# Cross-attention of 16 batches: K, V and Q projections moved from a stage of their own into the attention turns, each tile in two parts

## The chip, the cores and the metric

One NeuronCore of a Trainium2 chip runs the whole kernel. Its engines are TensorE (PE, whose weight loads are shown as PEld), VectorE (DVE), ScalarE (ACT) and GpSimd (POOL); SyncE (SP) issues nearly all DMAs. The metric is the device time of one execution in microseconds (us), the median of several.

## What is computed

```python
q = split_heads(x @ w_q)                     # x: 16 x 256 x 320, 20 heads of 16
k, v = split_heads(text @ w_k), split_heads(text @ w_v)   # text: 248 tokens of 512
out_text = softmax(q k^T / 4) v
out_ip   = softmax(q k_ip^T / 4 + mask_ip) v_ip           # the last 8 tokens, with a mask from boxes
out = (merge(out_text) + merge(out_ip)) @ w_out + b_out + x
```

All is float32. The large projections are computed as three products of rounded parts (high x high, low x high, high x low).

## The kernel before, in words

**Projections.** The 16 batches are taken as 8 groups of two (512 columns). A group has ten tiles, 0 to 9: three of K (`k_tile`, L628, 12 matmuls of 512 columns), four of V (`v_tile`, L636, 12 of 320), three of Q (`q_tile`, L642, 8 of 512). `three` (L624 to L627) issues the three products of a chunk, and there are four chunks of the 512 context channels. The inputs arrive by DMA (`load_c`, `load_x`) and are split into a high part on ACT (`split_c` L406, `split_x` L411) and a low part on DVE (L513, L517, L519). A finished K or Q tile is split the same way (ACT L417, DVE L525) and a V tile is copied out (ACT L425, L427); SP stores them to DRAM. The tiles of this stage rotate over five PSUM banks (`ring`). After group 0 come the eight special tokens of all batches (`special`, L694), and on DVE the box mask (`mask`, L484 to L500, 22 small instructions in a chain), which POOL stores (L375) to `aux_rows`.

**Attention.** Then come turns, one for each batch b, of ten pairs of heads, p = 0 to 9. In pair p of turn b PE issues the key scores of batch b (`key_scores`, L716, into the two banks `score_t`), the query scores of the *next* batch (`query_scores`, L666, into `score_q`, two banks for even and two for odd pairs), at even p the product with V for a group of four heads (`values`, L730, bank `pv`), at odd p from 3 on a piece of the output projection of batch b-1 (`project_out`, L739, bank `pj`). ACT takes the exponential of the key scores (L471), and after even pairs it copies `pv` out (L462). DVE takes row maxima of the query scores (`maxima`, L534 and L536); the maxima go through DRAM (`store_rows`, `load_rows`) and come back as rows of the stacked q operand before the key scores of that batch. DVE also turns and inverts the sums (L586, L589), turns back (L594), and adds the residual (L601); POOL scales (L387, L392).

**What sets the order.** Every engine runs its own list, written by hand, with waits on semaphores. Each engine's `batch` function is the list of a turn; the tables `VALUES`, `EVACUATE`, `INVERT`, `TURN_BACK`, `OUT`, `FINISH` say at which pair what is done. Batches 2 to 13 and groups 1 to 6 are loops (`Fori`). The ten query scores of batch 0 stand between the tiles of the last group (`FIRST_SCORES`). The stacked operands of a batch (`load_stack`, seven DMAs, L278, L281, L285) are loaded two turns ahead into one of three buffers.

```python
            def key_scores(t, p):
                if p % HALF == 0:
                    pe.wait_ge(rows_loaded[p // HALF], 16 * (t.b + 1))
                need(pe, exp_done, PAIRS * t.b + p)
            ...
            def values(b, u, k):
                need(pe, o_evac, QUADS * b + k)
                pe.wait_ge(exp_done, PAIRS * b + 2 * (k + 1))
```

## Time and profile before

| | |
|---|---|
| runs, median (lowest to highest) | 556.62 us (554.52 to 559.1), 3 runs |
| the profiled execution | 556.4 us, of which the span in the trace is 554.6 us |
| mean granted clock of TensorE | 0.972 |
| busy share of the span: PE, DVE, ACT, POOL | 87%, 69%, 51%, 23% |
| DMA | 112.49 MB, 203 GB/s over the span |

A busy share is an average over stages: the first third of the span is nearly all PE, the rest is shared between PE, DVE and ACT. The profiled execution was 1.8 us longer than its span and lies at the median of the runs.

### The profile page before, as it was taken

What the parts mean: (1) busy time and instruction counts of PE and PEld (TensorE: products, weight loads), DVE (VectorE), ACT (ScalarE), POOL (GpSimd) and SP (SyncE); (2) the same over time, 40 slices, a digit from 0 to 9 for tenths busy, and PEclk for the clock granted to TensorE, in tenths of its full rate; (3) what the DMA queues carried; (4) which work ended last, traced back from release to release, by engine and by line L of the source; (5) the groups of instructions that cost most, each with busy time, mean ns of one, the idle gap of its engine ahead of it and who ended that gap; (6) DMA issues with size and microseconds to landing.
All of it is one profiled execution on the core that took longest, in us unless ns stands there. A gap on an engine that the chain in (4) does not pass through costs nothing.

```text
span 554.6 us, 12517 instructions
## 1 busy us (share of the span) xinstructions
PE 481.5 (87%) x4304; PEld 323.7 (58%) x4304; DVE 384.9 (69%) x706; ACT 280.3 (51%) x355; POOL 127.9 (23%) x205
## 2 busy tenths in 40 slices
PE   3979899999999586799799889897987988989985
PEld 2868687887887463455455555554554555555542
DVE  2739425325325256899779989897997999999932
ACT  3633335344344013666556666565664666666671
POOL 6014000000000000432323332331332433332341
PEclk9989999999999787999979999999998999999999
DMA  8978888888788935672681762672754654763211
GB/s 271 362 266 149 259 298 273 309 268 293 272 261 270 345 120 179 200 243 74 204 261 33 247 221 89 234 233 79 235 170 154 219 154 144 245 204 103 72 52 47
DMA packets 94195, 112.49 MB, mean 203 GB/s; under 512 B 14304, under 2 KB 72992, under 8 KB 94144
## 3 DMA queue, kind: packets, MB, share of 16 engines
q1 hardware_dynamic: 93296, 109.89, 60.6%
q0 software_dynamic: 848, 1.90, 1.9%
q8 instruction: 33, 0.54, 0.4%
q14 instruction: 18, 0.15, 0.1%
HBM read 73.17 MB, written 38.63 MB: 202 GB/s over the span
## 4 chain that ended last, share of the span: by engine, by line
PE 48%; DMA 15%; issue 11%; SPq 10%; DVE 9%; ACT 4%; POOL 3%; DVEq 0%; ACTq 0%; POOLq 0%
PE pv L730 10%; DMA max_rows<-row_buf 10%; PE score_t L716 5%; PE pj L739 4%; PE score_q L666 3%; ACT probs L471 3%; SPq L278 3%; PE score_t L625 3%; PE score_t L626 3%; PE score_t L627 3%; SPq L285 2%; PE pj L625 2%; DMA q_stack<-max_rows 2%; PE pj L627 2%; PE pj L626 2%
## 5 line engine op out<-in xcount | busy, mean ns | idle before, releaser
L534 DVE TENSOR_REDUCE max_cols<-score_q 128x4 fp32r<-128x992 f32 x160 | 187.1, 1170 | 46.4 <-PE score_q L666 41.1
L471 ACT ACTIVATE probs<-score_t 128x1024 f32<-128x1024 f32 x160 | 163.4, 1021 | 72.0 <-PE score_t L716 71.9
L730 PE MATMUL pv<-probs,v_cur 128*32 128x256 f32 x1920 | 124.5, 394 | 0.6 <-ACT probs L471 0.6
L387 POOL TENSOR_TENSOR o_turned<-o_turned,inv_cols 128x256 f32<-128x256 f32 x80 | 49.8, 622 | 179.7 <-DVE inv_cols L589 179.7
L716 PE MATMUL score_t<-q_stack,k_stack 64*128 64x256 f32 x440 | 56.5, 335 | 29.4 <-ACT probs L471 17.6
L730 PEld LDWEIGHTS pv<-probs,v_cur 128*32 128x32 f32 x1920 | 55.3, 111 | 41.1 <-issue 4.6
L462 ACT ACTIVATE o_all<-pv 128x512 f32<-128x512 f32 x80 | 47.8, 598 | 60.7 <-PE pv L730 60.7
L716 PEld LDWEIGHTS score_t<-q_stack,k_stack 64*128 64x128 f32 x440 | 33.8, 189 | 74.8 <-ACT probs L471 37.7
L739 PE MATMUL pj<-wo_sb,o_all 128*128 128x320 f32 x192 | 69.0, 468 | 2.9 <-DVE o_all L594 2.2
L381 POOL TENSOR_TENSOR x_all<-x_all,bias_sb 128x640 f32<-128x640 f32 x16 | 24.9, 1554 | 192.5 <-DMA x_all<-in_x 192.5
L586 DVE STREAM_TRANSPOSE o_turned<-o_all 128x512 f32<-128x512 f32 x80 | 56.1, 702 | 11.9 <-ACT o_all L462 11.9
L666 PE MATMUL score_q<-k_stack,q_stack 64*128 64x256 f32 x440 | 47.2, 293 | 12.1 <-DVE max_cols L536 7.0
L513 DVE TENSOR_TENSOR stack<-o_all,stack 128x1024 fp32r<-128x1024 f32 x16 | 19.0, 1222 | 54.3 <-ACT stack L406 54.3
L666 PEld LDWEIGHTS score_q<-k_stack,q_stack 64*128 64x128 f32 x440 | 35.7, 195 | 15.0 <-DVE max_cols L536 6.9
L739 PEld LDWEIGHTS pj<-wo_sb,o_all 128*128 128x128 f32 x192 | 31.1, 188 | 18.7 <-DVE o_all L594 3.9
L392 POOL TENSOR_TENSOR o_all<-o_turned 128x128 f32<-128x128 f32 x80 | 36.7, 459 | 9.3 <-POOL o_turned L387 5.5
L716 PE MATMUL score_t<-stack 64*128 64x256 f32 x200 | 25.2, 330 | 10.6 <-ACT probs L471 7.0
L716 PEld LDWEIGHTS score_t<-stack 64*128 64x128 f32 x200 | 15.0, 184 | 31.3 <-ACT probs L471 16.1
L536 DVE TENSOR_REDUCE max_cols<-score_q 128x4 fp32r<-128x32 f32 x160 | 28.8, 180 | 0.0
L417 ACT ACTIVATE qk_out<-score_t 128x512 fp32r<-128x512 f32 (+1 forms) x24 | 13.9, 593 | 24.8 <-PE score_t L627 14.4
L625 PE MATMUL pj<-stack,wk_hl 128*128 128x512 f32 x32 | 13.8, 430 | 11.4 <-DVE stack L513 11.4
L525 DVE TENSOR_TENSOR qk_out<-score_t,qk_out 128x512 fp32r<-128x512 f32 (+1 forms) x24 | 15.8, 681 | 9.6 <-ACT qk_out L417 9.6
(134 smaller groups left out, 719.5 us busy)
## 6 DMA issues: line engine op xcount, KB each, us to landing
q_stack<-q_parts SPq DMA_DIRECT2D x33, 320.0 KB, 4.5
k_stack<-k_parts SPq DMA_DIRECT2D x33, 320.0 KB, 5.6
v_rows<-v_out SPq DMA_DIRECT2D x32, 320.0 KB, 2.4
v_cur<-v_rows SPq DMA_DIRECT2D x16, 640.0 KB
o_all<-in_ctxT SPq DMA_DIRECT2D x16, 512.0 KB, 5.2
q_parts<-qk_out SPq DMA_DIRECT2D x32, 256.0 KB, 2.5
k_parts<-qk_out SPq DMA_DIRECT2D x32, 248.0 KB, 4.7
x_all<-in_x SPq DMA_DIRECT2D x16, 320.0 KB, 3.3
```

Of the source, the lines that this page charges most:

```text
L387: pool.tensor_tensor(out, out, inv_cols[:, k, :].unsqueeze(2).broadcast_to([P, 2 * S // 32, DH]), ALU.mult).then_inc(scaled, 1)
L392: pool.tensor_tensor(o_norm_t[:, k // 2, :, half:half + DH], out[:, 0:S // 32, :], out[:, S // 32:, :], ALU.add).then_inc(o_added, 1)
L462: nc.scalar.activation(o_raw[:, k, :], pv[:, :], ACT.Copy)\
L471: nc.scalar.activation(probs[:, slot(u, p), :], score_t[:, :], ACT.Exp, scale=SCALE)\
L534: nc.vector.tensor_reduce(out=max_cols[:, h, :, at:at + 4:2].rearrange("p t e -> p e t"), in_=both[:, :, :, 0:TEXT], op=ALU.max, axis=AX.X ...
L536: nc.vector.tensor_reduce(out=max_cols[:, h, :, at + 1:at + 4:2].rearrange("p t e -> p e t"), in_=both[:, :, :, TEXT:KEYS], op=ALU.max, ax ...
L586: nc.vector.transpose(turned_blocks(k), o_raw[:, k, :].rearrange("p (j n) -> p j n", n=32))\
L625: mm(out, w_hi, x_hi_, start=start, stop=False)
L666: last = mm(score_bank(first, p, e)[:, tile * KEYS:(tile + 1) * KEYS], q_cols(w, p, e, tile * P, P), k_cols(w, p, e, 0, KEYS), start=True, ...
L716: last = mm(score_t[:, 512 * e + S * tile:512 * e + S * tile + S], k_cols(t.w, p, e, tile * P, P), q_cols(t.w, p, e, 0, S), start=True, st ...
L730: last = mm(pv[32 * t:32 * t + 32, at:at + S], values_of(u, kind, 4 * k + t), probs[:, slot(u, 2 * k + t // 2), a:a + S], start=kind != 1, ...
L739: last = mm(pj[:, 0:D], o_norm[:, u, c, t * P:t * P + P], wo_sb[:, c, :], start=c == 0, stop=c == OC - 1)
```

## The change

- **Alone stage.** Only tiles 0 to 14 (group 0, and K and the first two V tiles of group 1) are still projected ahead of attention, over the five banks. On DVE the mask now stands behind tiles 10 to 12 and not ahead of them.
- **Turn -1.** A new turn of ten pairs without key scores holds the query scores of batch 0 and tiles 15 to 19.
- **Hosting turns.** Turns -1 to 11 host five tiles each: an even turn the three K tiles and two V tiles of group (t + 4) / 2, the odd turn after it the other two V tiles and the three Q tiles. A tile's first two chunks are issued at the end of an odd pair, its other two at the even pair that follows, ahead of `values`. A Q tile has three matmuls in its first part and five in its second. ACT and DVE take the tile one pair later (`tile_due`). The two c halves of the next group are split at pairs 6 and 8 (ACT) and 6 and 9 (DVE) of odd turns; x at pairs 3 and 4 of even turns.
- **PSUM.** Hosted tiles use two banks of `score_q`, so that the query scores have one pair of banks, not two, until pair 3 of turn 12: a query score then waits for the maxima of the pair before it.
- **SBUF.** c and x of groups 2 to 7 come through one buffer `raw` of 1536 columns: each of the three loads (c half 0, c half 1, x) waits until the one before it has been split. `c_hi` and `c_lo` have buffers of their own; `o_raw` and `o_turned` have three slots, not five.
- **SP.** A turn's list also has the tile stores and the c or x loads; the stack's K rows and Q rows are loaded apart. `load_rows` of the first half now stands behind the store of the turn's second tile.
- **Code.** All loops are unrolled.

```diff
+SLOTS = 3
+TILES = 10
+LONE = 15
+LAST_HOST = B - 5
...
-        def score_bank(first, p, e):
-            at = 512 * (e + (0 if first else 2 * (p % 2)))
+        def pair_at(b, p):
...
-            at = 0 if first else 1024 * (p % 2)
+        def score_pair(b, p):
+            at = pair_at(b, p)
             return score_q[:, at:at + 1024].rearrange("p (e t n) -> p e t n", e=2, t=2)
-        ring = [pj[:, :], pv[:, :], score_t[:, 0:512], score_t[:, 512:1024], score_q[:, 1536:2048]]
+        lone_banks = [pj[:, :], pv[:, :], score_t[:, 0:512], score_t[:, 512:1024], score_q[:, 1536:2048]]
+        host_banks = [score_q[:, 1024:1536], score_q[:, 1536:2048]]
+        def tile_bank(n):
+            return lone_banks[n % 5] if n < LONE else host_banks[n % 2]
...
+            return 0 <= b < B
+        def hosted(t):
+            return -1 <= t <= LAST_HOST
+        def tile_due(t, p):
+            if p % 2 == 0:
+                return None
+            n = 5 * (t + 4) + (p - 3) // 2
+            return n if (hosted(t) if p > 1 else hosted(t - 1)) else None
+        def tile_freed(eng, n):
...
+            def load_c(g, h):
+                if g < 2:
                     need(sp, c_split, 2 * g + h - 1)
-                    sp.dma_start(c_raw[:, 2 * h:2 * h + 2, :], rows(ctxT[h * 256:h * 256 + 256, bass.ds(g * GT, GT)]))\
-                        .then_inc(c_loaded[h], 16)
+                elif h == 0:
+                    need(sp, x_tail, g if g > 2 else 0)
+                    sp.wait_ge(c_split, 2 * g)
+                else:
+                    sp.wait_ge(c_split, 2 * g + 1)
+                sp.dma_start(c_raw(g, h), rows(ctxT[h * 256:h * 256 + 256, g * GT:(g + 1) * GT]))\
+                    .then_inc(c_loaded[h], 16)
...
+            sp.wait_ge(ksp_stored, 96)
+            sp.wait_ge(sp_stored, 16)
+            sp.wait_ge(aux_stored, 64)
+            load_stack_k(0)
+            load_stack_q(0)
+            lone(12, 14)
...
+                if t >= 0:
                     load_rows(t, 1)
-                if t.there(-2):
-                    store_out(b - 2)
-                load_residual(b, u)
+                if hosted(t - 1) or t == -1:
+                    store_tile(5 * (t + 4) - 1)
+                if host and t % 2 == 0:
+                    load_x(g)
+                if host and t % 2 and g + 1 < GROUPS:
+                    load_c(g + 1, 0)
                 if ahead:
-                    scored(t, 0)
-                    load_stack(t.to(2))
+                    need(sp, st_ready, PAIRS * t)
+                    load_stack_k(t + 2)
                 if next_:
-                    need(sp, pv_ready, QUADS * b)
-                    load_values(b + 1, 1 - u)
-                    store_rows(b + 1, 0)
-                    load_rows(t.to(1), 0)
-                    store_rows(b + 1, 1)
-            def store_out(b):
-                need(sp, out_done, OT * (b + 1))
-                sp.dma_start(rows(out[bass.ds(b * S, S), :]), out_sb[:, :, :]).then_inc(out_stored, 16)
-            batches(sp, batch, tail=False)
+                    need(sp, pv_ready, QUADS * t)
+                    load_values(t + 1)
+                if there(t - 2):
+                    store_out(t - 2)
+                if t >= 0:
+                    load_residual(t)
+                if host:
+                    store_tile(5 * (t + 4))
+                if ahead:
+                    load_stack_q(t + 2)
+                if next_:
+                    store_rows(t + 1, 0)
+                if host:
+                    store_tile(5 * (t + 4) + 1)
+                if next_:
+                    load_rows(t + 1, 0)
+                if host and t % 2 and g + 1 < GROUPS:
+                    load_c(g + 1, 1)
+                if host:
+                    store_tile(5 * (t + 4) + 2)
+                    store_tile(5 * (t + 4) + 3)
+                if next_:
+                    store_rows(t + 1, 1)
+            for t in range(-1, B):
+                batch(t)
...
+                    n = tile_due(t, p) if t >= 0 or p != 1 else LONE - 1
+                    if n is not None:
+                        tile(n)
...
+                    if hosted(t) and t % 2 and g + 1 < GROUPS and p in SPLIT_C_HI:
+                        split_c(g + 1, SPLIT_C_HI[p])
+                    if hosted(t) and t % 2 == 0 and p == SPLIT_X_HI:
+                        split_x(g)
+            batch(-1)
...
+            tile(10)
+            split_x(1)
+            tile(11)
+            tile(12)
+            mask()
+            dve.wait_ge(preset, 8)
...
+                    n = tile_due(t, p) if t >= 0 or p != 1 else None
+                    if n is not None:
+                        tile(n)
...
+                    if hosted(t) and t % 2 and g + 1 < GROUPS and p in SPLIT_C_LO:
+                        split_c(g + 1, SPLIT_C_LO[p])
+                    if hosted(t) and t % 2 == 0 and p == SPLIT_X_LO:
+                        split_x(g)
...
+                alone = pair_at((n - 1) // PAIRS, (n - 1) % PAIRS) == pair_at(b, p)
+                need(pe, max_done, n if alone else n - 1)
...
+                if chunks[0] == 0:
+                    if j == 7:
                         pe.wait_ge(x_tail, g + 1)
...
+                    if n < LONE:
+                        if n >= 5:
+                            tile_freed(pe, n - 5)
                     else:
-                        q_tile(g, n - 7, out)
-                    if isinstance(g, int) and g == GROUPS - 1:
-                        for p in FIRST_SCORES.get(n, ()):
-                            query_scores(Turn(0, 0), p)
-                if first:
-                    special()
+                        tile_freed(pe, n - (1 if n == LONE else 2))
...
+            for n in range(TILES):
+                tile(n)
+            special()
+            for n in range(TILES, LONE):
+                tile(n)
+            pe.wait_ge(ksp_lo, 3)
+            pe.wait_ge(vsp_done, 1)
...
-                            query_scores(t.to(1), p)
+                    if there(t + 1):
+                        query_scores(t + 1, p)
+                    if p % 2 == 0 and (hosted(t) if p else hosted(t - 1)):
+                        tile(5 * (t + 4) + p // 2 - 1, (2, 3))
...
+                    if hosted(t) and p % 2:
+                        tile(5 * (t + 4) + p // 2, (0, 1))
+            for t in range(-1, B + 1):
+                batch(t)
...
-FIRST_SCORES = {3: [0, 1], 4: [2], 5: [3], 6: [4], 7: [5, 6], 8: [7], 9: [8, 9]}
+SPLIT_C_HI, SPLIT_C_LO = {6: 0, 8: 1}, {6: 0, 9: 1}
+SPLIT_X_HI, SPLIT_X_LO = 3, 4
```

Three places of the order show it. **TensorE, pairs 7 and 8 of an attention turn, before** (`score_t` key scores, `score_q` query scores, `pj` output projection, `pv` values):

```order
L716 MATMUL score_t<-q_stack,k_stack 128x256 x4
L666 MATMUL score_q<-stack 128x256 x4
L739 MATMUL pj<-wo_sb,o_all 128x320 x2
L716 MATMUL score_t<-q_stack,k_stack 128x256 x4
L666 MATMUL score_q<-stack 128x256 x4
L730 MATMUL pv<-probs,v_cur 32x256 x12
```

and now, the same pairs from the output projection on, in an odd turn with a Q tile (L645 to L647 and L673, L674 write it into a bank of `score_q`):

```order
L762 MATMUL pj<-wo_sb,o_all 128x320
L645 MATMUL score_q<-x_hi,wq_hi 64x512
L646 MATMUL score_q<-x_hi,wq_lo 64x512
L647 MATMUL score_q<-x_lo,wq_hi 64x512
L739 MATMUL score_t<-q_stack,k_stack 128x256 x4
L689 MATMUL score_q<-stack2 128x256 x4
L645 MATMUL score_q<-x_hi,wq_hi 64x512
L646 MATMUL score_q<-x_hi,wq_lo 64x512
L647 MATMUL score_q<-x_lo,wq_hi 64x512
L673 MATMUL score_q<-x_hi,wq_hi 64x512
L674 MATMUL score_q<-x_hi,wq_lo 64x512
L753 MATMUL pv<-probs,v_cur 32x256 x12
```

The part of a tile stands between the output projection and the next key scores, and between the query scores and the values. **VectorE, pairs 5 to 7 of an attention turn, before** (`max_cols` maxima, `c_lo` the low part of c):

```order
L586 STREAM_TRANSPOSE o_turned<-o_all 128x512 [waits o_added,o_evac]
L589 RECIPROCAL inv_cols<-o_turned 128x16 [waits turned]
L534 TENSOR_REDUCE max_cols<-score_q 128x2x2 [waits sq_ready]
L536 TENSOR_REDUCE max_cols<-score_q 128x2x2
L601 TENSOR_TENSOR out_sb<-pj,x_all 128x320 [waits biased,out_ready]
```

and now, pairs 6 and 7 of an odd hosting turn:

```order
L558 TENSOR_REDUCE max_cols<-score_q 128x2x2 [waits sq_ready]
L560 TENSOR_REDUCE max_cols<-score_q 128x2x2
L613 TENSOR_TENSOR out_sb<-pj,x_all 128x320 [waits biased,out_ready]
L534 TENSOR_TENSOR c_lo<-raw,c_hi 128x1024 [waits c_high]
L558 TENSOR_REDUCE max_cols<-score_q 128x2x2 [waits sq_ready]
L560 TENSOR_REDUCE max_cols<-score_q 128x2x2
L549 TENSOR_TENSOR qk_out<-score_q,qk_out 128x512 [waits hi_done]
L598 STREAM_TRANSPOSE o_turned<-o_all 128x512 [waits o_added,o_evac]
L601 RECIPROCAL inv_cols<-o_turned 128x16 [waits turned]
```

The low split of c, which waits for ACT (`c_high`), stands ahead of the maxima of pair 7. **VectorE at the end of the alone stage, now** (`o_turned` the special keys, `qk_out` the low parts of tiles 10, 11, 12, then the first of the mask):

```order
L586 TENSOR_TENSOR o_turned<-score_q,o_turned 64x128 [waits ksp_hi]
L549 TENSOR_TENSOR qk_out<-pj,qk_out 128x512 [waits hi_done]
L538 TENSOR_TENSOR x_lo<-o_all,x_hi 128x1024 [waits x_high]
L540 TENSOR_TENSOR x_hi<-o_all,x_hi 64x512
L549 TENSOR_TENSOR qk_out<-pv,qk_out 128x512 [waits hi_done]
L549 TENSOR_TENSOR qk_out<-score_t,qk_out 64x512 [waits hi_done]
L512 TENSOR_SCALAR x_all<-x_all,boxes 16x256 [waits loaded_boxes]
```

Before, the mask's first instruction followed the special keys directly.

## Rows read from the trace of the kernel before

**Rows 1.** Windows by stage: us, busy (count) by engine, granted clock, DMA share, GB/s
```profile
42.70:180.70 138.00, 136.00 (x698) 111.21 (x696) 62.55 (x87) 55.06 (x83) 4.77 (x7) 1.00 0.84 266
...
186.00:211.70 25.70, 19.95 (x100) 15.04 (x102) 13.64 (x22) 3.28 (x6) 0.00 (x0) 0.81 0.59 202
...
233.70:525.20 291.50, 258.28 (x2970) 151.40 (x2970) 260.08 (x515) 177.68 (x210) 96.92 (x154) 0.98 0.53 172
525.20:554.60 29.40, 21.41 (x208) 11.04 (x208) 10.72 (x27) 13.27 (x16) 9.03 (x15) 0.99 0.15 48
```

**Rows 2.** Timeline of PE, an even and an odd pair: start us, duration us
```profile
342.54 0.51 PE L716 MATMUL score_t<-q_stack,k_stack 64*128 64x256 f32 x4 [0.96 <-ACT probs L471]
...
342.88 0.40 PE L666 MATMUL score_q<-k_stack,q_stack 64*128 64x256 f32 x4
...
343.21 1.50 PE L730 MATMUL pv<-probs,v_cur 128*32 128x256 f32 x24
...
344.64 0.50 PE L716 MATMUL score_t<-q_stack,k_stack 64*128 64x256 f32 x4
...
345.31 1.34 PE L739 MATMUL pj<-wo_sb,o_all 128*128 128x320 f32 x4
...
346.58 0.50 PE L716 MATMUL score_t<-q_stack,k_stack 64*128 64x256 f32 x4
```

**Rows 3.** Timeline of PE, first matmuls of two V tiles, then of two K tiles
```profile
98.86 0.31 PE L625 MATMUL pj<-wv_hl,stack 128*128 128x320 f32 x1
...
100.62 0.31 PE L625 MATMUL pv<-wv_hl,stack 128*128 128x320 f32 x1
...
107.88 0.40 PE L625 MATMUL pj<-stack,wk_hl 128*128 128x512 f32 x1
...
110.67 0.39 PE L625 MATMUL pv<-stack,wk_hl 128*128 128x512 f32 x1
```

**Rows 4.** Timeline of PE, last group: a V tile between two query scores
```profile
192.35 0.50 PE L666 MATMUL score_q<-k_stack,q_stack 64*128 64x256 f32 x4
...
192.78 0.42 PE L625 MATMUL pj<-wv_hl,stack 128*128 128x320 f32 x1
...
194.74 0.50 PE L666 MATMUL score_q<-k_stack,q_stack 64*128 64x256 f32 x4
```

**Rows 5.** Timeline: first matmul of tile 10, first and last instruction of the mask
```profile
42.73 0.39 PE L625 MATMUL pj<-stack,wk_hl 128*128 128x512 f32 x1
```
```profile
40.79 0.55 DVE L490 TENSOR_SCALAR x_all<-x_all,boxes 16x256 f32<-16x256 f32 x1
...
52.91 0.28 DVE L500 TENSOR_SCALAR v_cur<-x_all 16x256 f32<-16x256 f32 x1
```

**Rows 6.** First load of batch 0's stack (SP), and the query scores that waited
```profile
173.93 2.09 SPq L278 DMA_DIRECT2D q_stack<-q_parts  x3
...
186.01 0.79 PE L666 MATMUL score_q<-k_stack,q_stack 64*128 64x256 f32 x4 [5.12 <-DMA k_stack<-k_parts]
```

**Rows 7.** DMA issues: KB each, median us from issue to landing
```profile
o_all<-in_ctxT SPq DMA_DIRECT2D x16, 512.0 KB, 5.2
...
aux_rows<-v_cur POOLq DMA_DIRECT2D x2, 80.0 KB, 3.3
```

**Rows 8.** Groups of 80 to 180 us: the splits of c, count, busy, mean ns
```profile
L513 DVE TENSOR_TENSOR stack<-o_all,stack 128x1024 fp32r<-128x1024 f32 x10 | 11.8, 1222 | 38.0 <-ACT stack L406 38.0
L406 ACT ACTIVATE stack<-o_all 128x1024 fp32r<-128x1024 f32 x10 | 10.0, 1051 | 0.0
```

**Rows 9.** Timeline of attention: copy-out of pv, maxima of a pair, an exponential
```profile
344.86 0.60 ACT L462 ACTIVATE o_all<-pv 128x512 f32<-128x512 f32 x1 [0.74 <-PE pv L730]
...
345.35 1.02 ACT L471 ACTIVATE probs<-score_t 128x1024 f32<-128x1024 f32 x1
345.42 1.19 DVE L534 TENSOR_REDUCE max_cols<-score_q 128x4 fp32r<-128x992 f32 x1
346.53 0.18 DVE L536 TENSOR_REDUCE max_cols<-score_q 128x4 fp32r<-128x32 f32 x1
```

598 lines of the change are left out of this document (270 added, 328 removed).

## The prediction

> **What bounds the kernel now.** I read the windows by stage first [rows 1]. Three stages stand in them. From 42.7 to 180.7 us only projections run: PE is busy 136.0 of 138.0 us at clock 1.00, DVE and ACT under half. From 186.0 to 211.7 the last tiles and the first query scores share PE, which is busy 19.95 of 25.7 us at clock 0.81. From 233.7 to 525.2 run 14 attention turns, 291.5 / 14 = 20.8 us each, PE busy 258.3 of 291.5. So a PE-bound stage stands beside one where PE has gaps, and the change wants to fill the gaps with the tiles. What they are worth is read from the timeline of a pair [rows 2]. Key scores to query scores 0.34 us, query scores to values 0.33, values to the next key scores 344.64 - 343.21 = 1.43: an even pair is 2.10 us of PE. An odd pair with four matmul records of output projection is 1.94 (1.27 from 345.31 to 346.58). A turn's PE work is 10 x 0.67 + 5 x 1.43 + 12 records of output projection at 1.27 / 4 = 3.8, together 17.7 us. The turn takes 20.8: only 3.1 us of it are gaps.
>
> **Hosted work on PE.** A V tile is 100.62 - 98.86 = 1.76 us, a K tile 110.67 - 107.88 = 2.79 [rows 3], so 0.2325 for a matmul of 512 columns and 8 x 0.2325 = 1.86 for a Q tile. A group is 3 x 2.79 + 4 x 1.76 + 3 x 1.86 = 21.0, half a group in a turn 10.5 on average. A turn's last tile is finished in pair 0 of the next, so an even turn has the second part of a Q tile (5 x 0.2325 = 1.16), three K tiles, a V tile and half a V tile: 17.7 + 1.16 + 8.37 + 1.76 + 0.88 = 29.8 us. An odd turn has half a V tile, two V tiles, two Q tiles and the first part of a third (0.70): 26.5. So PE alone makes a hosting turn 28 on average, not 20.8. The gain has to come from the 138 us that vanish ahead of them.
>
> **What a part costs beyond its matmuls.** The trace has one place where a tile stands between scores: from a query score to the next with one V tile between, 194.74 - 192.35 = 2.39 us [rows 4]. Less 1.76 and less the 0.34 of query scores in rows 2, 0.3 is left for two changes between kinds of matmul, 0.15 for one. A part adds one net change to its pair. Ten parts: 1.5 us in each turn. Bounds: 0 (PE's queue hides it) and 0.3 for each, 3.0 a turn. I take 0.15, the nearest row.
>
> **The start.** Up to tile 10 nothing changes: 42.7 us [rows 5]. Tiles 10 to 14: 3 x 2.79 + 2 x 1.76 = 11.9, to 54.6. On DVE the mask now waits for tile 12, whose matmuls end at 42.7 + 8.4 = 51.1; its high and low copy cost about 0.6 and 0.8 (estimated from the 512-column copy of rows 9), so the mask starts near 52.6 and takes 53.2 - 40.8 = 12.4 [rows 5]: 65.0. Its two stores by POOL land 3.3 after issue [rows 7], about 1 us for the issues: 69.4. Only then SP may load batch 0's stack. Before, the first load issue and the first query score stood 186.0 - 173.9 = 12.1 us apart with a second stack's loads mixed in [rows 6]; alone I take 10 (bounds 7.5, the seven issues and one landing, and 12.1). Turn -1 starts at 79.5: PE stands still for 25 us. Before, this wait was hidden under six groups of tiles.
>
> **Turn -1.** With one pair of banks its clock is the loop query scores (0.4 to 0.8) and maxima, 346.71 - 345.42 = 1.29 [rows 9], with handovers near 2.0 us, ten times; two c splits of 1.2 on DVE [rows 8], and a clock that was 0.81 in the like stretch before [rows 1]. I take 22.5 (bounds 20 and 25.7): turn 0 starts at 102, where before it started at 211.7. That is 110 us earlier. In return 60 of the 80 tiles, 12 x 10.5 = 126 us of PE, lie in turns 0 to 11, which have gaps of 12 x 3.1 = 37 us for them.
>
> **The hosting turns.** Turn 0 has no values of an earlier batch and no output projection: 29.8 - 1.4 - 3.8 + 1.5 = 26. Turns 1 to 11 (six odd, five even): 6 x 26.5 + 5 x 29.8 + 11 x 1.5 = 324.5. On top come two waits, which I follow through the engines' lists. ACT and DVE take their lists in order.
> - Odd turn, pair 6: values end 0.67 + 1.16 + 0.15 + 1.43 = 3.4 us into the pair; ACT copies `pv` out (0.15 later, 0.6 [rows 9]), only then splits c (1.05 [rows 8]), to 5.2; DVE, at the head of whose queue the low split waits, ends it at 6.45. Behind it stand the maxima of pair 7, to 7.7, and for these the query scores of pair 8 now wait, as they have one pair of banks; they were due at 3.4 + (0.67 + 1.27 + 0.70 + 0.15) + 0.34 = 6.5. Cost 1.25.
> - Pair 8: the second half of c is loaded only after that split, issue near 6.6 and landing 5.2 later [rows 7], 11.8; ACT splits it to 12.6 or later, and the exponential of pair 9 (1.02) stands behind: key scores of the next turn at 13.75, due at 12.9. Cost 0.85. DVE's low split, then maxima: query scores of the next pair 1 late by 1.1.
> - Together 3.2 in each of the five odd turns that split (1, 3, 5, 7, 9): 16. Bounds: 0, if the slack of other pairs takes it, and 6 each (30), if landings take 3 us more. The x split in even turns comes out within 0.3 of its cover (load issued after the last Q tile's store, near 10 us into the turn, split due at 13.5): 1.5 in all.
>
> DVE and ACT by themselves have room: DVE's added work is (six lows of 0.7, two c splits, an x split) near 4.2 us a turn on about 18.5 of busy time, under 28.
>
> [...]
>
> **The end.** Turns 12 to 14 as before, 3 x 20.8 = 62.4; the last 29.4 [rows 1] unchanged.
>
> **Sum.** 102 + 26 + 324.5 + 16 + 1.5 + 62.4 + 29.4 = 561.8 of span, against 554.6; with the 1.8 us around the span 563.6, so 563. The profiled execution, 556.4, lies at the median of the runs, 556.6. Break-even is a mean of (554.6 - 102 - 62.4 - 29.4) / 12 = 30.1 us over turns 0 to 11; I have 368 / 12 = 30.7.
>
> **Rivals.**
> - *PE hides the waits.* The changes of kind cost nothing, and the c split's waits are taken by slack: and turn -1 takes 20.5: 563 - 16.5 - 16 - 2 = 528; with half of it true, 546. For it: 136.0 of 138.0 us busy in the dense stage, and waits of PE in the turns before were few. Against: rows 4, and the list order on DVE.
> - *The single raw buffer decides (slower).* c half 1 and x are loaded only when the part before is split, and the engines stand with exponentials and maxima behind them. With the landing at 8 us, not 5.2 and near 4 for x (stack loads, values and tile stores now share the DMA queues), each odd turn loses 3 more and each even turn 2.5: 5 x 3 + 5 x 2.5 = 27, 590; with half of it 577. It decides from a landing of about 5 us after issue. For it: 12.1 us for a stack in rows 6. Against: the DMA share would be near 0.7, below the 0.84 of the projection stage, where 5.2 was measured.
> - *The clock.* PE restarts after 25 us of rest, and turn -1 has it busy about 60%. If the low clock, 0.81 on average in rows 1, lasts through turn 0, it adds 5: 568.
> - *The change doesn't overlap at all* (a wait holds each tile until attention has finished its pair): turns of 20.8 + 10.5 = 31.3, 12 x 31.3 = 376 in place of 368: 571.
>
> **How the numbers follow.** Forecast, a little slower, 551 to 575: chance 0.46, near half of it within 1% of the median. First rival 0.32, all of it faster than 551. Raw buffer 0.16, slower. The last two together 0.06, a third of it within 1%. So faster by over 1% 0.32, within 1% 0.26, slower by over 1% 0.42; one per cent is about what runs of this kernel can tell from no change. Range 538 to 584: it leaves out the deep end of the first rival (528 to 538) and the deep end of the second.
>
> **What would show it.** Tile 14 ends near 54.6 and PE then waits for a DMA till about 79.5. Turn 0's key scores start near 102. Even hosting turns near 31, odd ones near 30, with PE or PEld waiting for maxima in pair 8, for an exponential in the next pair 0, and for maxima in pair 1. In pairs without split, PE waits for nothing. Wrong would be: a start of turn 0 beyond 108 or before 96; waits of ACT for `raw` of over 2 us; a mean hosting turn under 29 or over 32; a granted clock under 0.97 in turns 1 to 11.

## The result, and the profile after

The changed kernel takes 566.99 us (median of 4 runs, 564.82 to 570.51), the kernel before 557.42 beside it (554.52 to 559.1): ratio 1.022, 95% interval 1.016 to 1.027. It is slower by about 2%; the forecast was 563.0, range 538 to 584. The profiled execution took 566.87, its span is 565.1, its mean granted clock 0.96.

Windows of the changed kernel by stage answer to [rows 1]: us, then busy time (count) of PE, PEld, DVE, ACT, POOL, then granted clock, DMA share, GB/s.

```profile
54.60:79.50 24.90, 1.88 (x15) 1.64 (x13) 9.56 (x24) 0.96 (x2) 1.01 (x2) 0.58 0.41 125
79.50:99.60 20.10, 16.55 (x85) 11.22 (x85) 14.24 (x22) 2.90 (x5) 0.00 (x0) 0.84 0.80 271
99.60:128.90 29.30, 27.21 (x238) 17.23 (x237) 22.19 (x38) 16.72 (x22) 4.70 (x7) 1.00 0.70 218
128.90:466.50 337.60, 326.94 (x2921) 211.62 (x2921) 248.12 (x459) 180.06 (x236) 79.81 (x121) 1.00 0.67 212
466.50:491.70 25.20, 21.37 (x218) 11.97 (x218) 19.72 (x38) 13.22 (x17) 6.80 (x11) 0.93 0.58 181
491.70:533.70 42.00, 36.34 (x424) 21.43 (x425) 37.54 (x75) 25.35 (x30) 13.72 (x22) 1.00 0.40 125
533.70:565.10 31.40, 23.39 (x208) 11.87 (x208) 10.77 (x27) 13.27 (x16) 9.00 (x15) 0.87 0.14 44
```

The rows are the hole at the start, turn -1, turn 0, turns 1 to 11, turn 12, turns 13 and 14, and the end. In turns 1 to 11 TensorE is busy 326.9 of 337.6 us at a granted clock of 1.00: it is the bound there, as it was under the dense projections in [rows 1]. The lengths, each from the key scores of pair 0 to those of the next turn, against the forecast's terms:

| stretch | forecast | measured | difference |
|---|---|---|---|
| start of turn 0 | 102 | 99.6 | -2.4 |
| turn 0 | 26 | 29.3 | +3.3 |
| turns 1 to 11 | 324.5 + 16 + 1.5 = 342 | 337.6 | -4.4 |
| turns 12 to 14 | 62.4 | 67.2 | +4.8 |
| the last stretch | 29.4 | 31.4 | +2.0 |
| span | 561.8 | 565.1 | +3.3 |

The terms miss by 16.9 us in all, and by 3.3 after they cancel: that the sum lies so near is in part luck. Before, turns 12 to 14 took 20.56 + 19.68 + 19.78 = 60.0 us by the starts of their key scores, not the 62.4 of the mean turn, so against the kernel before they are 7.2 us longer, not 4.8.

The hole at the start, in the timeline of the changed kernel (start us, duration us, what it waited for): last step of the mask, SyncE's first stack load, its last, and the first query score.

```profile
64.69 0.28 DVE L522 TENSOR_SCALAR v_cur<-x_all 16x256 f32<-16x256 f32 x1
...
68.56 1.99 SPq L276 DMA_DIRECT2D k_stack<-k_parts  x3
...
72.60 0.62 SPq L272 DMA_DIRECT2D q_stack<-aux_rows  x1
...
79.46 0.80 PE L689 MATMUL score_q<-k_stack,q_stack 64*128 64x256 f32 x4 [23.02 <-DMA q_stack<-aux_rows]
```

The mask ends at 65.0 and the first query score comes at 79.46: forecast 65.0 and 79.5. Between them two small misses cancel: the stack load is issued at 68.6, not 69.4, and the query score comes 10.9 us after it, not 10. Before, the like load stood under a queue of projection tiles [rows 6]; now TensorE stands 23 us.

The waits that the forecast followed through the lists, in turn 1 (its pair 8 begins at 151.5, turn 2 at 159.0):

```profile
149.51 1.05 ACT L421 ACTIVATE c_hi<-raw 128x1024 fp32r<-128x1024 f32 x1
150.59 1.23 DVE L534 TENSOR_TENSOR c_lo<-raw,c_hi 128x1024 fp32r<-128x1024 f32 x1 [2.70 <-ACT c_hi L421]
151.74 1.19 DVE L558 TENSOR_REDUCE max_cols<-score_q 128x4 fp32r<-128x992 f32 x1
152.16 0.44 SPq L214 DMA_DIRECT2D raw<-in_ctxT  x1
153.07 0.50 PE L689 MATMUL score_q<-stack 64*128 64x256 f32 x4 [1.04 <-DVE max_cols L560]
...
159.03 0.50 PE L739 MATMUL score_t<-stack 64*128 64x256 f32 x4 [0.56 <-ACT probs L483]
160.92 1.16 DVE L534 TENSOR_TENSOR c_lo<-raw,c_hi 128x1024 fp32r<-128x1024 f32 x1
162.15 1.15 DVE L558 TENSOR_REDUCE max_cols<-score_q 128x4 fp32r<-128x992 f32 x1
...
163.46 0.50 PE L689 MATMUL score_q<-k_stack,q_stack 64*128 64x256 f32 x4 [0.51 <-DVE max_cols L560]
```

Read it from the DVE row at 150.59: VectorE stood 2.70 us for ScalarE's `c_hi` with the maxima of pair 7 behind it, and the query scores of pair 8, which have one pair of banks, then stood 1.04. The two other waits follow at pair 0 and pair 1 of the next turn, where the forecast had them. But the first of these does not come from the load, as the forecast had it. ScalarE's rows, and the load of `raw` (KB, us from issue to landing):

```profile
156.43 0.60 ACT L475 ACTIVATE o_all<-pv 128x512 f32<-128x512 f32 x1 [3.33 <-PE pv L753]
156.93 1.05 ACT L421 ACTIVATE c_hi<-raw 128x1024 fp32r<-128x1024 f32 x1
```
```profile
raw<-in_ctxT SPq DMA_DIRECT2D x1, 512.0 KB, 3.7
```

Issued at 152.16, the second half of c landed near 155.9. ScalarE waited for the values to copy `pv` out, split c right behind, and took the exponential of pair 9 after that. The load was in time; the copy-out of `pv` set the start, as it did at pair 6. Pairs by the starts of their key scores (us):

| pair | with c splits (turn 3) | without (turn 11) | cost | forecast |
|---|---|---|---|---|
| 8 | 4.76 | 3.46 | 1.30 | 1.25 |
| 9 | 2.74 | 2.10 | 0.64 | 0.85 |
| 1 of the next turn | 3.07 | 2.26 (run e3) | 0.81 | 1.1 |

The stretch that the forecast had wrong is turn 12, the first without tiles. Before, the last turns took 19.7 to 20.6 us; now turn 12 takes 25.2. Its rows in the changed kernel:

```profile
471.74 0.51 SPq L253 DMA_DIRECT2D q_stack<-max_rows  x1
472.78 1.15 SPq L239 DMA_DIRECT2D q_parts<-qk_out  x2
474.10 1.96 SPq L276 DMA_DIRECT2D stack<-k_parts  x3
...
477.18 0.40 SPq L297 DMA_DIRECT2D out<-out_sb  x1
...
484.45 0.49 DVE L613 TENSOR_TENSOR out_sb<-pj,x_all 128x320 f32<-128x320 f32 x1 [2.23 <-issue]
485.00 2.23 PE L762 MATMUL pj<-wo_sb,o_all 128*128 128x320 f32 x4 [2.41 <-DVE out_sb L613]
487.16 0.80 PE L739 MATMUL score_t<-q_stack,k_stack 64*128 64x256 f32 x4
```

SyncE issues the store of batch 10's output at 477.18, 10.7 us into the turn, behind a maxima load, the store of tile 79 and a stack load. VectorE's next residual sum writes the same `out_sb`; by its list it waits for that store, though the row names no releaser for its 2.23 us. It starts at 484.45, and the output projection stands 2.41 us for it. The key scores after the wait take 0.80, not 0.51, at a granted clock of 0.50 (window 487.0 to 488.0); over the turn it is 0.93, where it had been 1.00.

### The profile page after: what moved, and what is told of

It reads as the page before. It is cut to its first block, busy times and chain, and to the rows that moved or that the text cites. A ratio compares the mean times of both kernels' runs of the same rounds, so it can differ in the third digit from the quotient of the medians.

```text
span 565.1 us, 11048 instructions
## 1 busy us (share of the span) xinstructions
PE 495.4 (88%) x4304; PEld 321.7 (57%) x4304; DVE 385.0 (68%) x706; ACT 274.6 (49%) x355; POOL 131.8 (23%) x206
## 3 DMA queue, kind: packets, MB, share of 16 engines
q0 software_dynamic: 944, 2.23, 2.2%
## 4 chain that ended last, share of the span: by engine, by line
issue 56%; POOL 19%; PE 8%; DMA 6%; DVE 6%; SPq 3%; ACT 1%; POOLq 0%; ACTq 0%; DVEq 0%
POOL o_turned L402 9%; POOL o_all L407 6%; POOL x_all L396 4%; DMA probs<-in_wv_ip 3%; DVE max_cols L558 2%; PE score_q L689 1%; DMA v_rows<-v_out 1%; PE score_q L645 1%; DMA q_stack<-aux_rows 1%; DVE x_all L514 1%; PE score_q L646 1%; PE score_q L647 1%; DVE c_lo L534 1%; PE pj L762 1%; PE pv L753 1%
## 5 line engine op out<-in xcount | busy, mean ns | idle before, releaser
L753 PE MATMUL pv<-probs,v_cur 128*32 128x256 f32 x1920 | 120.4, 383 | 0.6 <-ACT probs L483 0.6
L402 POOL TENSOR_TENSOR o_turned<-o_turned,inv_cols 128x256 f32<-128x256 f32 x80 | 53.9, 674 | 165.9 <-DVE inv_cols L601 165.9
L762 PE MATMUL pj<-wo_sb,o_all 128*128 128x320 f32 x192 | 71.7, 484 | 5.9 <-DVE out_sb L613 3.9
L598 DVE STREAM_TRANSPOSE o_turned<-o_all 128x512 f32<-128x512 f32 x80 | 56.1, 701 | 11.8 <-ACT o_all L475 11.8
L762 PEld LDWEIGHTS pj<-wo_sb,o_all 128*128 128x128 f32 x192 | 32.2, 194 | 22.3 <-DVE out_sb L613 5.4
L645 PE MATMUL score_q<-wv_hl,c_hi 128*128 128x320 f32 x112 | 43.0, 384 | 0.0
L646 PE MATMUL score_q<-wv_hl,c_lo 128*128 128x320 f32 x112 | 35.1, 313 | 0.0
L647 PE MATMUL score_q<-wv_hl,c_hi 128*128 128x320 f32 x112 | 35.0, 312 | 0.0
L645 PE MATMUL score_q<-c_hi,wk_hl 128*128 128x512 f32 (+1 forms) x72 | 33.1, 460 | 0.0
L549 DVE TENSOR_TENSOR qk_out<-score_q,qk_out 128x512 fp32r<-128x512 f32 (+1 forms) x40 | 27.4, 684 | 7.3 <-ACT qk_out L442 5.8
L534 DVE TENSOR_TENSOR c_lo<-raw,c_hi 128x1024 fp32r<-128x1024 f32 x14 | 16.8, 1202 | 22.3 <-ACT c_hi L421 22.3
```

The costliest lines, as they stand in the source:

```text
L402: pool.tensor_tensor(out, out, inv_cols[:, n % SLOTS, :].unsqueeze(2).broadcast_to([P, 2 * S // 32, DH]), ALU.mult).then_inc(scaled, 1)
L598: nc.vector.transpose(turned_blocks(n), o_raw[:, n % SLOTS, :].rearrange("p (j n) -> p j n", n=32))\
L645: mm(out, w_hi, x_hi_, start=start, stop=False)
L753: last = mm(pv[32 * t:32 * t + 32, at:at + S], values_of(u, kind, 4 * k + t), probs[:, slot(u, 2 * k + t // 2), a:a + S], start=kind != 1, ...
L762: last = mm(pj[:, 0:D], o_norm[:, b % 2, c, t * P:t * P + P], wo_sb[:, c, :], start=c == 0, stop=c == OC - 1)
```

## The experiments

All times are medians of 4 to 10 runs, each with the kernel before on the same chip beside it. The changed kernel was not run again beside them, so of the timed runs the ratio to the kernel before (1.022 for the changed kernel) is what compares, and what a step is worth is read from the traces, one for each kernel. Each edit is to the changed kernel (567.0) unless it says e8.

**e1: the mask first.**

```diff
-            tile(10)
-            split_x(1)
-            tile(11)
-            tile(12)
-            mask()
+            mask()
+            tile(10)
+            split_x(1)
+            tile(11)
+            tile(12)
...
-            lone(7, 12)
+            lone(7, 10)
...
-            lone(12, 14)
+            lone(10, 14)
```

> Against the changed kernel at 567.0: the mask goes ahead of projected tile 10 on VectorE, and SyncE stores tiles 10 to 13 behind the first stack load instead of ahead of it. Theory A (the first query score waits 23 us for the stack load, which waits for the mask, and nothing else is behind it): the first query score comes 10 to 11 us earlier, near 69, and every later turn starts that much earlier: about 556.5 us. Rival B (turn -1 is then held by something else, the second ctxT load or tiles 10 to 14 evacuated late): turn -1 grows by about what the start gains, 563 to 567.

Measured: 557.64, ratio to before 1.002 (0.997 to 1.006); span 553.9.

```profile
68.15 0.80 PE L689 MATMUL score_q<-k_stack,q_stack 64*128 64x256 f32 x4 [11.78 <-DMA q_stack<-aux_rows]
```

The first query score comes 11.3 us earlier and the span falls by 11.2. Theory A, but the two numbers agree by luck: turn 12 starts only 8.3 us earlier, and of the rest 2.0 is the last stretch, 29.4 us here and 31.4 in the changed kernel, which the mask doesn't touch. Turn 0 gave back 2.3 us (31.6, not 29.3): ScalarE's second split of c still waited for its load (5.83 us, at 89.52), with an exponential and the maxima behind it. The mask and SyncE's order were moved together; between them they decide whether the changed kernel is slower or level.

**e2: one split a pair earlier.**

```diff
-SPLIT_C_HI, SPLIT_C_LO = {6: 0, 8: 1}, {6: 0, 9: 1}
+SPLIT_C_HI, SPLIT_C_LO = {5: 0, 8: 1}, {6: 0, 9: 1}
```

> One number changes: ScalarE's first split of c goes to pair 5 instead of pair 6; VectorE's stays at pair 6. Theory A (the long pair 8 of each odd turn, 4.76 against 3.46 without splits, comes from VectorE's low split standing 2.7 us for ScalarE's high one, with the maxima behind it): that wait is gone, pair 8 of the odd turns 1 to 9 falls to about 3.5, the second half of ctxT is loaded some 2 us earlier, and the time falls by 5 x 1.3 = 6.5 to 8 us, to about 560. Rival B (ScalarE itself is the late one: its exponential of pair 6 moves behind the split and takes the wait over): pair 6 or 7 grows by about 1 us and the time stays within 2 us of 567.

Measured: 564.84, ratio 1.012 (1.003 to 1.020). Pair 8 of the odd turns fell from 4.76 to 3.46, just as theory A said; but pair 9 rose from 2.74 to between 2.85 and 3.14 (3.86 in turn 9), and turn 0 from 29.3 to 32.0. The wait named by theory A was real: with VectorE's split still at pair 6, it was ScalarE's place alone that took it away. Of the 6.5 us, pair 9 of the five turns took back 2.4 and turn 0 another 2.7. Neither theory had the number.

**e3: no splits.** Loads and splits of c and x return at once for groups 2 and up, with the waits for them.

> Leaves out, from group 2 on, the loads and the splits of ctx and x; every later projected tile is made from group 1's values, so this is a time only. Theory A (the splits cost their waits, 16 us in the odd turns and 1.5 in turn -1 and the even turns, as forecast): about 549.5 us, hosted turns all at 29 to 29.5. Rival B (TensorE is the bound and hides the splits; the odd turns with a split, 29.95, are only 2 us longer than turn 11 without one, 28.0): 5 x 2 + 5 x 0.5 = about 12 us less, 555. Rival C (their loads also hold up other transfers): under 545.

Measured: 548.97, ratio 0.983 (0.975 to 0.992). Window of turns 1 to 11 in this run:

```profile
126.10:449.90 323.80, 323.80 (x2922) 210.88 (x2921) 228.26 (x439) 163.85 (x221) 75.58 (x121) 1.00 0.60 193
```

TensorE is busy 323.80 of 323.80: without splits and their loads it waits for nothing, so all of the difference to 337.6, 13.8 us, is the price of the two there. Another 2.8 is in turns -1 and 0. Odd turns take 28.0 and even ones 31.1 here; the forecast had 28.0 and 31.3. Theory A in size.

**e4: stores ahead in turns 12 to 15.**

```diff
+                if not host:
+                    store_out(t - 2)
+                    load_residual(t)
                 if t >= 0:
                     load_rows(t, 1)
...
-                if there(t - 2):
+                if host and there(t - 2):
                     store_out(t - 2)
-                if t >= 0:
+                if host and t >= 0:
                     load_residual(t)
```

> In the turns without projected tiles (12 to 15) SyncE stores the output of two turns ago and loads the residual before it loads maxima rows and stacks; nothing else moves. Theory A (turn 12 takes 25.2 us, not 20.8, because the late store of out_sb holds VectorE's residual sum, and with it the output projection, for 2.4 us, and the clock falls behind that wait): turn 12 falls to 21 to 22, the total by 3 to 4.5, to about 563. Rival B (turn 12 is long because of projected tile 79 and the single pair of score banks in its first pairs): turn 12 stays above 24 and the total within 1.5 us of 567.

```profile
471.20 0.38 SPq L297 DMA_DIRECT2D out<-out_sb  x1
...
467.80:490.10 22.30, 19.81 (x218) 11.26 (x217) 20.56 (x41) 13.22 (x17) 6.92 (x11) 1.00 0.66 204
```

The store goes out 3.4 us into the turn; turn 12 takes 22.3 us, not 25.2, at clock 1.00, and turn 13 takes 19.75, not 22.2, without a wait of 1.97 us for maxima rows at its end. Turns 12 to 14 together take 61.8 us, 5.4 less. The span is 560.7, 4.4 less, for turn 12 started 1.3 us later in this execution. Store and residual load were moved together. The timed median, 565.19 (ratio 1.016, 1.004 to 1.027), fell by less, and its interval holds both 0 and 4.4: the mechanism is shown by the trace, its size only there.

**e5 and e6: whole tiles.** The parts (2, 3) and (0, 1) become one call for all four chunks, in e5 at the even pair, in e6 at the odd pair.

```diff
 # e5
-                        tile(5 * (t + 4) + p // 2 - 1, (2, 3))
+                        tile(5 * (t + 4) + p // 2 - 1)
...
-                    if hosted(t) and p % 2:
-                        tile(5 * (t + 4) + p // 2, (0, 1))
```

> Each projected tile is made whole at the even pair where its second part stood; the odd pairs carry none. Theory A (a change of kind of matmul costs TensorE 0.15 to 0.2 us, as the forecast had it, and there are five fewer of them per hosted turn): 12 turns x 0.75 to 1.0 = 9 to 12 us less, about 556, with the saving seen in the sum of an odd and the even pair that follows. Rival B (the odd pairs, now short of work, fall to the floor of the query scores' single pair of banks, 0.33 + 1.3 + the semaphores, about 1.9, while the even pairs take the tile whole): pairs sum to the same and the time is 565 to 568. Rival C (the even pairs, with 4.9 us of work, keep ScalarE and VectorE idle, and splits and evacuations bunch behind them): 572 or more.

> Each projected tile is made whole at the odd pair where its first part stood; the even pairs carry none. Theory A (fewer changes of kind): 9 to 12 us less than 567, about 556. Rival B (TensorE does the same matmuls wherever they stand): 565 to 568. Rival C (the first key tile of an even turn now needs all of c at pair 1, while its second half is split only at pair 9 and pair 0: a new wait of 1 to 2 us in 5 turns): 570 to 575.

Measured: e5 606.33, ratio 1.085 (1.078 to 1.093); e6 559.92, ratio 0.999 (0.995 to 1.003). I had not expected the one to be 46 us from the other: for e5 only rival C had the direction, with no number near it. Timeline of PE in e5, turn 11, an even pair's end and the odd pair behind it:

```profile
475.98 1.50 PE L753 MATMUL pv<-probs,v_cur 128*32 128x256 f32 x24
477.42 0.51 PE L739 MATMUL score_t<-stack 64*128 64x256 f32 x4
477.76 0.39 PE L689 MATMUL score_q<-k_stack,q_stack 64*128 64x256 f32 x4
479.12 0.50 PE L739 MATMUL score_t<-stack 64*128 64x256 f32 x4 [0.96 <-ACT probs L483]
```

An odd pair has 0.67 us of work, or 1.3 to 1.9 with output projection, and no values. The key scores of the next pair need its exponential (1.02 us and the handovers), 1.70 us after its own. Without a part in it TensorE stands 0.96. The even pair has values to fill that time; a whole tile there covers what was covered already. So turn 11 takes 30.2 in e5 and the odd turns with splits 33.1 to 34.7. In e6 turn 11 takes 27.1 us, 0.9 under the changed kernel's 28.0, and TensorE is busy all of both. Windows of turn 11, of e6, then of the changed kernel:

```profile
438.90:466.00 27.10, 27.10 (x261) 18.38 (x260) 20.11 (x37) 14.83 (x20) 6.75 (x11) 1.00 0.60 202
```
```profile
438.50:466.50 28.00, 28.00 (x262) 18.53 (x261) 19.36 (x38) 14.77 (x20) 6.87 (x11) 1.00 0.60 200
```

That is 0.18 for each of five parts fewer. What e6 loses is at pair 1 of the even turns, 4.7 to 7.3 us, where the whole first key tile needs the second half of c (its rival C); even so its turns 1 to 11 take 331.6 us, 6.0 less. It loses more ahead of them: turn -1 takes 27.0 us, not 20.1. The profiled execution took 567.58, 7.7 above the median, so the traced loss is more than the timed runs show. The total hides a gain and two losses.

**e7: the splits where VectorE has room.**

```diff
-SPLIT_C_HI, SPLIT_C_LO = {6: 0, 8: 1}, {6: 0, 9: 1}
-SPLIT_X_HI, SPLIT_X_LO = 3, 4
+SPLIT_C_HI, SPLIT_C_LO = {5: 0, 9: 1}, {6: 0}
+SPLIT_X_HI, SPLIT_X_LO = 5, 6
...
+                    if hosted(t) and t % 2 == 0 and p == 0:
+                        split_c(g, 1)
```

> Only the places of the splits change: ScalarE splits c at pairs 5 and 9 instead of 6 and 8, VectorE at pair 6 and at pair 0 of the next turn instead of 6 and 9, and x at 5 and 6 instead of 3 and 4. Theory A (the splits cost only because VectorE's low split stands at an odd pair, beside an inversion of 0.95 us, with one pair of banks for the query scores, so that the maxima behind it come late; an even pair has room for it): pair 8 of odd turns 3.5, pair 9 2.1, pair 1 of even turns 2.3, the hosted turns near the 28.0 and 31.1 of the run without splits, so about 12 to 15 us less: 552 to 555. Rival B (what e2 showed, where pair 8 gained 1.3 and pair 9 lost 0.4 to 1.1: the load of the second half of c, 4 to 5 us behind VectorE's first split in one raw buffer, is late whatever the place): ScalarE stands for raw at pair 9 or 0 and the gain is under 5 us.

Measured: 552.83, ratio 0.988 (0.981 to 0.995). Its turns 1 to 11, and its first low split:

```profile
127.90:452.40 324.50, 324.44 (x2924) 211.04 (x2923) 253.93 (x459) 178.70 (x236) 87.34 (x121) 1.00 0.69 221
```
```profile
144.28 1.07 ACT L421 ACTIVATE c_hi<-raw 128x1024 fp32r<-128x1024 f32 x1
...
146.83 1.39 DVE L534 TENSOR_TENSOR c_lo<-raw,c_hi 128x1024 fp32r<-128x1024 f32 x1
```

All splits are back, and TensorE is busy 324.44 of 324.5. The low split waits for nothing and ends at 148.22, as pair 7's query scores start. With every load through the one raw buffer, 13.1 of the 13.8 us are gone: rival B, and with it the forecast's raw buffer rival, fall. What cost time was the place in the lists, of both engines. VectorE's first low split stands at pair 6 in both kernels: what helped it was that ScalarE's high split is done a pair earlier (e2 shows the same at pair 8). Only its second was moved, out of pair 9, which holds an inversion (0.95) beside maxima (1.3) in 2.1 us of TensorE, to pair 0, which like pair 6 lasts 3.4 to 3.5 us and has room; ScalarE's second split went a pair later with it, and the two were not tried apart.

**e8: the three together** (e1, e4, e7).

> The three edits together: the mask and its loads ahead (e1), stores and residual ahead in turns 12 to 15 (e4), splits moved (e7). Theory A (they touch different stretches and add up: e1's profiled span was 11.2 us under the changed kernel's, e4's 4.4, e7's 12 to 15 by its theory): about 537 to 541, faster than both kernels. Rival B (an earlier start puts turn -1 and 0 on loads that are not there yet, as in e1, where turn 0 took 2.3 us more, and e7 gains under 5): 547 to 551.

Measured: 538.97, ratio 0.965 (0.961 to 0.970): faster than both kernels. The gains of the three spans, 11.2 + 4.4 + 12.9 = 28.5, add up to its 28.9 (565.1 - 536.2). By stretches they do too, more loosely: turn 12 starts 8.3 us earlier in e1, 14.1 in e7 and 23.7 here, and turns 12 to 14 are 5.4 shorter in e4 and 5.6 here. The last stretch, 31.7, gained nothing.

**e9 and e10: e8 with whole tiles.** A tile is whole at its odd pair unless the pair is in a set; e9: pair 1 of even turns; e10: pairs 5 and 9 of odd turns, 1 and 5 of even ones.

> The joined version (e8, 539.0) with the tiles whole at the odd pairs, but for the first tile of an even turn, which stays in two parts. Theory A (a change of kind costs TensorE 0.18, as turn 11 showed: busy 28.00 in two parts, 27.10 whole at the odd pairs; nothing else is lost): 11 or 12 turns x 0.7 to 0.9, about 9 us less: 530. Rival B (room moves with the tile: an even pair falls to 2.10, so VectorE's low splits of c at pairs 6 and 0 no longer fit behind the maxima, 1.29 + 1.22 and 0.43 to 0.49 more, and each costs TensorE about 1 us): 10 of them and 6 splits of x give back 9 to 16: 539 to 546.

> The joined version (e8) with whole tiles at the odd pairs, but in two parts where the even pair that follows holds a low split: pairs 5 and 9 of odd turns, 1 and 5 of even turns. Theory A (0.18 per change of kind, and the splits keep the room they have in e8): 3 changes fewer in each turn, 11 or 12 x 0.54 = 6 to 6.5 us less than e8: about 533. Rival B (the odd pairs with a whole key tile and the even ones at 2.10 break the rhythm of evacuations, maxima late once or more a turn): 539 or more. By both, e10 against e9 tells whether room for the split or the count of parts decides.

Measured: e9 536.73, ratio 0.968 (0.962 to 0.974); e10 533.70, ratio 0.962 (0.956 to 0.968). An odd and an even turn together take 59.1 in e8, 58.2 in e9, 57.8 in e10. At 0.18 a change e9 has 9 fewer in two turns, 57.5, and e10 6 fewer, 58.0. So e10 keeps its gain in these turns, as its theory A said; e9 loses 0.7 of its own, between its two theories. In turns 1 to 11 of e9 TensorE waits for maxima at pair 9 of the five even turns (0.18 to 0.39 us), on a VectorE that is late from the x splits, and its weight load four times at pair 2 (0.26 to 0.27), behind the low split of c; in e10 it never waits: room for the splits is worth more than the last three changes. Both lose in turn -1, which no theory had. Windows of turn -1, of e8, then of e10:

```profile
69.05:89.68 20.63, 17.05 (x83) 11.57 (x83) 14.22 (x22) 3.11 (x5) 0.00 (x0) 0.81 0.89 296
```
```profile
67.64:94.39 26.75, 21.12 (x84) 15.26 (x84) 14.31 (x22) 4.16 (x6) 0.00 (x0) 0.59 0.74 255
```

With whole tiles it takes 6.1 us more in e10 and 8.9 more in e9: TensorE stands longer for maxima where a pair has no part (1.39 us each time), and the granted clock over the turn is 0.59 in e10, not 0.81. Parts in turn -1 and whole tiles behind it were not tried.

**e11 and e12: e8 with one more cut.** In e11 chunk 0 goes ahead of the output projection and chunk 1 behind it (odd pairs); in e12 chunk 2 goes ahead of the values and chunk 3 behind them (even pairs).

```diff
 # e12
-                        tile(5 * (t + 4) + p // 2 - 1, (2, 3))
+                        tile(5 * (t + 4) + p // 2 - 1, (2,))
...
+                    if p % 2 == 0 and (hosted(t) if p else hosted(t - 1)):
+                        tile(5 * (t + 4) + p // 2 - 1, (3,))
```

> The joined version (e8, 539.0) with the part of an odd pair cut once more: its first c chunk ahead of the output projection, its second behind (in three of four odd pairs of key and value tiles; a query tile's part moves ahead whole). More pieces, but output projection and tile use the array alike (128*128 in the rows), so the shape the array is used in changes no more often than in e8. Theory A (the 0.18 is paid when the shape changes, 64*128 scores, 128*32 values, 128*128 tiles): no change, 538 to 541, odd turns 28.0. Rival B (it is paid by each piece of a tile): 3 or 4 pieces more in each of 12 turns, 7 to 9 us more, 546 to 548.

> The joined version (e8) with the part of an even pair cut once more: its first c chunk ahead of the values, its second behind them. Five more changes of shape in each hosted turn (128*128 to 128*32 and back to 128*128). Theory A and rival B of e11 both expect 0.18 for each: 60 x 0.18 = 10.8 us more, near 550, with TensorE busy throughout; so that e12 without e11 longer is theory A, and both longer is B. Rival C (the 0.18 of the whole tiles was a wait and not a change of shape): both stay at 539.

Measured: e11 536.61, ratio 0.961 (0.955 to 0.967), 1.4 us under its theory A; e12 548.81, ratio 0.981 (0.975 to 0.987). Turn 11: 28.02 in e8, 27.96 in e11, 28.99 in e12. Windows of turns 1 to 11, of e8, then of e12:

```profile
118.80:442.80 324.00, 324.00 (x2921) 210.91 (x2921) 252.44 (x459) 178.41 (x236) 86.85 (x121) 1.00 0.70 221
```
```profile
119.70:454.20 334.50, 334.50 (x2924) 208.56 (x2923) 252.79 (x460) 184.58 (x236) 86.99 (x121) 1.00 0.67 214
```

TensorE does the same matmuls and is never idle in both, yet is busy 10.5 us longer: 55 cuts at 0.19. More pieces beside output projection cost nothing (27.96), so what counts is the shape at the cut. In pair 3 of turn 11 of e11 the pieces of the tile and the output projection between them all have 128*128:

```profile
421.85 0.50 PE L744 MATMUL score_t<-stack 64*128 64x256 f32 x4
...
422.91 0.31 PE L652 MATMUL score_q<-wv_hl,c_hi 128*128 128x320 f32 x1
423.06 1.24 PE L767 MATMUL pj<-wo_sb,o_all 128*128 128x320 f32 x4
423.90 0.55 PE L650 MATMUL score_q<-wv_hl,c_hi 128*128 128x320 f32 x1
...
424.67 0.51 PE L744 MATMUL score_t<-stack 64*128 64x256 f32 x4
```

The step from the tile to the output projection is 0.15, as inside the tile, and the pair takes 2.82 us, as in e8. In the rows of an even pair of e8 the neighbours have other shapes:

```profile
426.55 0.41 PE L650 MATMUL score_q<-wv_hl,c_hi 128*128 128x320 f32 x1
426.80 0.31 PE L651 MATMUL score_q<-wv_hl,c_lo 128*128 128x320 f32 x1
426.95 0.31 PE L652 MATMUL score_q<-wv_hl,c_hi 128*128 128x320 f32 x1
...
427.39 0.31 PE L652 MATMUL score_q<-wv_hl,c_hi 128*128 128x320 f32 x1
427.62 1.50 PE L758 MATMUL pv<-probs,v_cur 128*32 128x256 f32 x24
```

Matmuls of one shape start 0.15 apart; from 64*128 scores the first takes 0.25, and to the 128*32 values the step is 0.23: 0.10 + 0.08. So going into the tile's shape and out again costs 0.18 us here; what TensorE does in that time, no row shows. And not every change costs: the third Q tile uses the array as 128*64. Behind two records of output projection, rows of turn 11 of the changed kernel, first with a 128*128 part (pair 5), then with a 128*64 part (pair 9), each to the next key scores:

```profile
453.42 0.81 PE L762 MATMUL pj<-wo_sb,o_all 128*128 128x320 f32 x2
...
454.86 0.51 PE L739 MATMUL score_t<-stack 64*128 64x256 f32 x4
```
```profile
465.09 0.81 PE L762 MATMUL pj<-wo_sb,o_all 128*128 128x320 f32 x2
...
466.52 0.50 PE L739 MATMUL score_t<-q_stack,k_stack 64*128 64x256 f32 x4
```

It is 1.44 and 1.43 us: going on from 128*128 to 128*64 costs nothing that the rows show.

## Why the prediction was right, point by point

- *The start.* Right in mechanism: mask end 65.0, turn -1 at 79.5, with 0.8 too much before the stack load and 0.9 too little behind it. e1 shows the cause, the mask with SyncE's order; it costs 11 us at the first query score.
- *Turn -1* took 20.1, at the lower bound, not 22.5; *turn 0* took 29.3, not 26. I put both c splits of turn -1 into turn -1; the second was split at 99.2, in turn 0, and cost 2.2 us there (e3: 27.1). Of the other 1.1, most is that turn 0 has no output projection: its four odd parts from pair 3 on stand alone between scores, where each adds a change (0.2; pair 3 took 2.27, worked out 0.67 + 1.40 + 0.20). Together 0.9 us off, as the two misses nearly cancel.
- *What a part costs.* Mis-sized in its step "a part adds one net change to its pair": a change into another shape and out costs 0.18 to 0.20, so 0.15 was near, but a part beside output projection adds none (pair 3 of turn 11 took 2.82, which is 0.67 + 1.27 + 0.88). Five even parts and the one in pair 1 make 1.1 us a turn, not 1.5. That turns without splits still came out at 28.0 and 31.1, forecast 28.0 and 31.3, is in part luck: the base was too low. The forecast charged output projection by the record, 1.27 / 4, but two records alone took 0.74 (453.42 to 454.86, less 0.70 for the part), not 0.64, twice a turn.
- *The c splits.* Right in place at all three pairs, and in mechanism at pair 8 and pair 1; 2.75 in each of the five odd turns, 13.8 together, forecast 16 (e3). At pair 9 the size was near (0.64, forecast 0.85), but the step that made its load the last wait ("landing 5.2 later") did not hold: it landed in 3.7 and was in time, and ScalarE came to it late, behind the copy-out of `pv`. By the forecast's own numbers that split would also end at 12.85, not 12.6. The x split cost nothing, forecast 1.5.
- *The end.* Wrong: "turns 12 to 14 as before". I followed what SyncE's list does to hosted turns and not to the first one without tiles, where store and residual loads still stand behind the last tile's store; e4 takes 5.4 us of turns 12 to 14 away, and what is left over the 60.0 before is 1.8, most of it the second part of tile 79 in pair 0 of turn 12 (3.4, not 2.1). The last 2 us are the clock: the last six output-projection matmuls take 3.57 us, 1.88 before, at a granted clock of 0.50 while they ran, 1.00 before (0.87 over the stretch, 0.99 before), with no other work moved. The change is not shown to be the cause: e1 and e11, which have it, end as the kernel before did. The six matmuls, before, in the changed kernel, and in e1:

```profile
549.44 1.88 PE L739 MATMUL pj<-wo_sb,o_all 128*128 128x320 f32 x6 [0.58 <-DVE out_sb L601]
```
```profile
558.24 3.57 PE L762 MATMUL pj<-wo_sb,o_all 128*128 128x320 f32 x6 [0.58 <-DVE out_sb L613]
```
```profile
548.78 1.88 PE L762 MATMUL pj<-wo_sb,o_all 128*128 128x320 f32 x6 [0.58 <-DVE out_sb L613]
```

- *Rivals.* That TensorE hides the waits: no, 13.8 us of splits and 1.1 a turn of changes are in the turns, though turn -1 did take 20.1. The raw buffer: in turns 1 to 11 ScalarE waited for it at most 2.22 us, five times for x, and TensorE lost nothing by it; once, ahead of turn 0, it waited 4.52, over the 2 us that the forecast named as a sign of wrong. e7 keeps the buffer, and its turns 1 to 11 take 0.7 us more than those of e3. The clock: 1.00 in turns 0 to 11, and 0.93 in turn 12, behind a wait. No overlap: a mean hosted turn of 30.6, but in e3 TensorE is busy in all of it.
- *One pair of banks for the query scores.* TensorE waits for maxima only where a split stands ahead of them, ten times and 7.8 us in turns 1 to 11; in e7, with the same one pair, never, and turn 11, without a split, is busy 28.00 of 28.00 us. In turn -1, where no key scores and values fill the pairs, it waits five times (0.31 to 1.46 us); query scores follow each other there every 1.89 us (88.42, 90.31, 92.20), less than the 2.10 of a plain even pair.

The change brought turn 0 forward by 112 us (from 211.7 to 99.6) and made the 12 turns from there on 9.5 us longer each, and it filled their gaps as it meant to (e3: TensorE is busy throughout turns 1 to 11). It lost the gain to four bills: 23 us of rest ahead of the first query score, 16.6 for splits placed badly in the lists of ScalarE and VectorE, 5.4 for a late store, and about 13 for changes of shape (12 turns x 1.1, worked out). The first three are a matter of order, and e8 has 28.9 us of them back. What is left of the rest at the start, 11.8 us in e1, was not tried.

## What to carry to other kernels

When dense work is spread into a paced loop, price first what stood hidden beneath the dense stage (here a mask and a stack load), then the place of each small helper in its engine's list: put it in the pair where that engine has room, which one sees by its busy time against the pair's length, and put what it waits for a pair ahead of it (e2). Work that fills gaps must go to the pairs that have them (e5 against e6), beside matmuls that use the array in the same shape (turn 11: 27.96 us with the cuts of e11, 28.99 with those of e12). And look at the first turn after the mixed ones: orders written for them may hold a store back.
